# The first transform of a four-layer spectral network on row tiles instead of column tiles of TensorE

## What is computed

```python
# x: (2, 64, 64, 384) float32; four layers, one after the other
x = _L0_conv_ref(x, L0_conv_w1, L0_conv_b1, L0_conv_w2, L0_conv_b2)
x = _L1_conv_ref(x, L1_conv_ln1_g, ..., L1_conv_mlp_b2)
x = _L2_conv_ref(x, L2_conv_w1r, ..., L2_conv_b2)
x = _L3_conv_ref(x, L3_conv_w1, ..., L3_conv_b2)

def _L0_conv_ref(x, w1, b1, w2, b2):          # 8 heads of 48 channels; layers 2 and 3 are of this kind
    xs = jnp.fft.rfft2(x, axes=(1, 2))
    xs = xs.reshape(B, H, W // 2 + 1, 8, 48)
    xr, xi = jnp.real(xs[:, lo:hi, :wk]), jnp.imag(xs[:, lo:hi, :wk])
    o1r = relu(einsum('bxyhi,hio->bxyho', xr, w1[0]) - einsum('bxyhi,hio->bxyho', xi, w1[1]) + b1[0])
    o1i = relu(einsum('bxyhi,hio->bxyho', xi, w1[0]) + einsum('bxyhi,hio->bxyho', xr, w1[1]) + b1[1])
    ...                                        # a second complex product, with w2 and b2
    out = softshrink(zr, 0.01) + 1j * softshrink(zi, 0.01)
    return jnp.fft.irfft2(out, s=(H, W), axes=(1, 2)) + x

def _L1_conv_ref(x, ln1_g, ln1_b, ln2_g, ln2_b, w1, b1, w2, b2, mlp_w1, mlp_b1, mlp_w2, mlp_b2):
    h = _ln(x, ln1_g, ln1_b)                   # layer norm over the channels
    h = afno2d(h, w1, b1, w2, b2) + x          # as above, first 32 of 64 rows of modes, gelu, no shrinking
    m = _ln(h, ln2_g, ln2_b)
    return _gelu(m @ mlp_w1 + mlp_b1) @ mlp_w2 + mlp_b2 + h
```

## Time and profile before

| | us |
|---|---|
| median of 3 runs | 2166.53 |
| lowest, highest | 2162.26, 2170.68 |
| the profiled execution's own time | 2166.18 |
| its span | 2164.1 |

### The profile page before, as it was taken

One profiled execution on the slowest core, in us unless ns is written; L12 is line 12 of the kernel. 1 busy time (PEld: TensorE's weight loads), 2 busy tenths in 40 slices (PEclk: granted clock), 3 DMA queues, 4 the chain that ended last, 5 costly groups with the idle time before them and its releaser, 6 DMA issues.

```text
span 2164.1 us, 76669 instructions
## 1 busy us (share of the span) xinstructions
PE 2056.5 (95%) x35424; PEld 1766.8 (82%) x35424; DVE 937.7 (43%) x1814; ACT 874.2 (40%) x1470; POOL 440.4 (20%) x425
## 2 busy tenths in 40 slices
PE   5999995999998999999999999999999999999997
PEld 4788873887885999999999999998787888877885
DVE  1354667875645433333333333331343443433443
ACT  2544445443443333333333333333444444444442
POOL 3211013975521110000000000001220220221200
PEclk9999997999999999999999999999999999999999
DMA  9425638306425111111111111114707257246314
GB/s 163 89 45 82 113 58 148 54 18 109 113 60 135 30 30 30 29 29 29 29 29 29 29 29 29 39 35 84 110 5 122 49 83 118 58 76 116 61 23 99
DMA packets 299726, 141.57 MB, mean 65 GB/s; under 512 B 275632, under 2 KB 298032, under 8 KB 299440
## 3 DMA queue, kind: packets, MB, share of 16 engines
q1 hardware_dynamic: 299440, 137.11, 34.9%
HBM read 74.17 MB, written 62.91 MB: 63 GB/s over the span
## 4 chain that ended last, share of the span: by engine, by line
PE 92%; DVE 3%; issue 2%; DMA 1%; SPq 1%; ACT 1%; POOL 0%; DVEq 0%; ACTq 0%; POOLq 0%
PE ps L578 19%; PE ps L563 19%; PE ps L466 11%; PE ps L436 10%; PE ps L450 9%; PE ps L485 8%; PE ps L420 8%; PE ps L500 7%; PE ps L548 1%; DMA xs<-in_x 1%; DMA wraw<-in_w 1%; DVE xn L827 1%; DVE st L807 1%; DVE mv L812 0%; DVE xn L829 0%
## 5 line engine op out<-in xcount | busy, mean ns | idle before, releaser
L436 PEld LDWEIGHTS ps<-const,z 128*48 128x48 f32 x8384 | 286.6, 124 | 102.5 <-issue 72.0
L910 DVE TENSOR_TENSOR gl<-g,gh 128x512 fp32r<-128x512 f32 x192 | 156.9, 817 | 476.5 <-ACT gh L719 476.5
L716 ACT ACTIVATE g<-ps,colp 128x512 f32<-128x512 f32 x192 | 132.4, 689 | 529.4 <-PE ps L563 529.4
L770 DVE TENSOR_SCALAR clamp<-ps 128x384 f32<-128x384 f32 (+1 forms) x216 | 113.2, 524 | 529.4 <-PE ps L466 529.3
L466 PE MATMUL ps<-w,h 113*64 113x48 f32 (+1 forms) x8384 | 285.4, 218 | 15.7 <-issue 14.4
L436 PE MATMUL ps<-const,z 128*48 128x64 f32 (+1 forms) x8384 | 283.3, 218 | 6.7 <-issue 4.6
L660 ACT ACTIVATE h<-ps,w 113x512 f32<-113x512 f32 (+2 forms) x280 | 171.1, 611 | 290.2 <-PE ps L450 290.2
L466 PEld LDWEIGHTS ps<-w,h 113*64 113x64 f32 (+1 forms) x8384 | 260.0, 131 | 23.0 <-issue 18.5
L420 PE MATMUL ps<-const,xn 128*64 128x64 f32 x6144 | 226.9, 228 | 45.3 <-POOL xn L996 21.2
L578 PE MATMUL ps<-w2h,gh 128*128 128x384 f32 x768 | 261.9, 341 | 0.0
L450 PE MATMUL ps<-zf,w 112*49 112x512 f32 (+5 forms) x1120 | 260.4, 528 | 0.6 <-issue 0.5
(11 more groups left out here) (67 smaller groups left out, 2392.9 us busy)
## 6 DMA issues: line engine op xcount, KB each, us to landing
after<-xs SPq DMA_DIRECT2D x96, 384.0 KB, 5.4
xs<-after SPq DMA_DIRECT2D x94, 384.0 KB, 8.8
after<-om SPq DMA_DIRECT2D x32, 384.0 KB, 4.3
out<-xs SPq DMA_DIRECT2D x32, 384.0 KB, 5.5
xm<-after SPq DMA_DIRECT2D x30, 384.0 KB, 6.3
xs<-in_x SPq DMA_DIRECT2D x24, 384.0 KB, 8.6
wstage<-in_spectral SPq DMA_DIRECT2D x16, 210.0 KB, 7.2
xs<-in_x SPq DMA_DIRECT2D x4, 768.0 KB, 11.6
```

What stands on the lines that cost most here:

```text
L436: mm = pe.matmul(ps[a * SIDE:a * SIDE + BLOCK, F2_BANK, n * L.kh:(n + 1) * L.kh], z[:, g % 2, slot, :], basis(col + a * SIDE, L.kh), start ...
L716: act.activation(g[:, n % 2, :], ps[:, MM1_BANKS[n % 2], :], ACT.Gelu, bias=colp[:, n:n + 1]).then_inc(g_ready, 1)
L910: dve.tensor_tensor(gl[:, n % 4, :], g[:, n % 2, :], gh[:, n % 4, :], ALU.subtract).then_inc(g_low, 1)
```

## The change

Two chunks of 8 channels become one *twin* of 16, three a group. The stationary tile is now 64 partitions (one image) x 128 columns (two channels, 64 rows h each); the moving operand is the 64 table columns on the same 64 partitions. The two images are two row tiles, which write banks 0 and 1 over all 128 partitions. The table `d1` is no longer block-diagonal: it is 64 columns, given once for each image. A twin has 16 matmuls; two chunks had 32.

The result has other places: partitions (channel parity j, h), columns (channel pair c, part a, k), bank b. `z` stays as it was, so ScalarE sorts: four copies of 64 partitions x 512 for a twin, of which two move data to the other half of the partitions. Each copy reads both banks, so the next `f1` waits for all four of the twin before. `f1_at` becomes [1, 4, 7] ([1, 4, 6] in layer 1); VectorE's `centre` keeps the old six places under the name `centre_at`.

```diff
@@ -30,6 +30,8 @@
 SPAN = BATCH * HALF
 CHAN = 8
 CHUNKS = BLOCK // CHAN
+TWINS = CHUNKS // 2
+SPREAD = 4
 ROWCHUNK = 8
 ROWCHUNKS = SIDE // ROWCHUNK
 PARTS = 4
@@ -40,7 +42,8 @@
 STATS = PAIRS + 1
 
 SIGNS = 5
-C_D1, C_D2, C_D2A, C_D2B, C_SIGN = [P * n for n in range(5)]
+C_D1 = 0
+C_D2, C_D2A, C_D2B, C_SIGN = [SPAN + P * n for n in range(4)]
 C_ID, C_D5, C_D5H, C_D6, C_COLS = [C_SIGN + SIGNS + P * n for n in range(5)]
 ROWS = ONE_ROW + 1
 MIX = SIDE + BLOCK
@@ -63,7 +66,8 @@
         self.groups = list(zip(starts, sizes))
         self.n = len(sizes)
 
-        self.f1_at = [0, 1, 3, 5, 7, 8] if self.full else [0, 1, 3, 4, 6, 7]
+        self.f1_at = [1, 4, 7] if self.full else [1, 4, 6]
+        self.centre_at = [0, 1, 3, 4, 6, 7]
         self.f5_at = [2, 3, 4, 5, 6, 7] if self.full else [1, 2, 3, 4, 5, 6]
 
     def column(self, slot):
@@ -406,26 +410,30 @@
             def f1(g, k):
 
                 L = layer_of(g)
-                n = CHUNKS * g + k
+                n = TWINS * g + k
+                chunk = 2 * n + 1
                 if L.norm and g == BLOCKS:
                     pe.wait_ge(rows_ready, SIDE)
                 elif L.norm:
-                    pe.wait_ge(xn_ready, n - CHUNKS * (BLOCKS + 1) + 1)
+                    pe.wait_ge(xn_ready, chunk - CHUNKS * (BLOCKS + 1) + 1)
                 else:
-                    pe.wait_ge(xt_ready, n + 1 - (CHUNKS * BLOCKS if L.index > 1 else 0))
-                if n >= 2:
-                    pe.wait_ge(z_ready, n - 1)
+                    pe.wait_ge(xt_ready, chunk + 1 - (CHUNKS * BLOCKS if L.index > 1 else 0))
+                if n >= 1:
+                    pe.wait_ge(z_ready, SPREAD * n)
                 for c in range(CHAN):
-                    for a in range(2):
-                        mm = pe.matmul(ps[a * SIDE:(a + 1) * SIDE, F1_BANKS[n % 2], c * SPAN:(c + 1) * SPAN],
-                                       xn[:, n % RING, c, :], basis(C_D1 + a * SPAN, SPAN), start=True, stop=True)
+                    slot, first = (chunk - 1 + c // (CHAN // 2)) % RING, c % (CHAN // 2) * 2
+                    for b in range(BATCH):
+                        rows = slice(b * SIDE, (b + 1) * SIDE)
+                        mm = pe.matmul(ps[:, F1_BANKS[b], c * SPAN:(c + 1) * SPAN],
+                                       xn[rows, slot, first:first + 2, :].rearrange("p c h -> p (c h)"),
+                                       const[rows, C_D1:C_D1 + SPAN], start=True, stop=True)
                 mm.then_inc(f1_done, 1)
 
             def f2(g, t):
 
                 L = layer_of(g)
                 if t == 0:
-                    pe.wait_ge(z_ready, CHUNKS * (g + 1))
+                    pe.wait_ge(z_ready, SPREAD * TWINS * (g + 1))
                     if g == 0:
                         pe.wait_ge(s_second, 16)
                         pe.wait_ge(gap_clear, 1)
@@ -504,7 +512,7 @@
 
             def spectral(first, last):
 
-                for k in range(CHUNKS):
+                for k in range(TWINS):
                     f1(first, k)
                 for g in range(first, last):
                     L = layer_of(g)
@@ -610,16 +618,19 @@
 
             def f1(g, k):
 
-                n = CHUNKS * g + k
-                act.wait_ge(f1_done, n + 1)
-                act.activation(z[:, g % 2, :, k * CHAN:(k + 1) * CHAN],
-                               ps[:, F1_BANKS[n % 2], :].rearrange("p (c s) -> p s c", s=SPAN),
-                               ACT.Copy, scale=layer_of(g).forward).then_inc(z_ready, 1)
+                act.wait_ge(f1_done, TWINS * g + k + 1)
+                for j, a in ((0, 0), (0, 1), (1, 1), (1, 0)):
+                    mine, to = slice(j * SIDE, (j + 1) * SIDE), slice(a * SIDE, (a + 1) * SIDE)
+                    first = 2 * k * CHAN + j
+                    act.activation(z[to, g % 2, :, first:first + 2 * CHAN - 1:2].rearrange("p (k b) c -> p k b c", b=BATCH),
+                                   ps[mine, F1_BANKS[0]:F1_BANKS[1] + 1, :]
+                                   .rearrange("p b (c a k) -> p a k b c", a=2, k=HALF)[:, a],
+                                   ACT.Copy, scale=layer_of(g).forward).then_inc(z_ready, 1)
 
             def normalise_row(r):
 
                 if r == 0:
-                    act.wait_ge(f1_done, CHUNKS * BLOCKS)
+                    act.wait_ge(f1_done, TWINS * BLOCKS)
                     act.wait_ge(x_loaded[buffer_of(PAIRS)], LOADS * (uses_before(PAIRS) + 1))
                 if r % ROWCHUNK == 0:
                     act.wait_ge(rstd_ready, r // ROWCHUNK + 1)
@@ -853,8 +864,8 @@
                             m2(g, t - 1)
                         elif g > first:
                             m2(g - 1, layer_of(g - 1).n - 1)
-                        if norm and t in L.f1_at:
-                            n = CHUNKS * (g + 1 - first) + L.f1_at.index(t) + AHEAD
+                        if norm and t in L.centre_at:
+                            n = CHUNKS * (g + 1 - first) + L.centre_at.index(t) + AHEAD
                             if n < CHUNKS * (last - first):
                                 centre(n)
                         if norm and 0 <= L.n * (g - last + 2) + t - 4 < HC:
@@ -992,14 +1003,14 @@
                         pool.wait_ge(x_loaded[buffer_of(unit)], LOADS * (uses_before(unit) + 1))
                 n = CHUNKS * g + k
                 if n >= RING:
-                    pool.wait_ge(f1_done, n - RING + 1)
+                    pool.wait_ge(f1_done, (n - RING) // 2 + 1)
                 pool.tensor_copy(xn[:, n % RING], channels(g, k)).then_inc(xt_ready, 1)
 
             def keep(n):
 
                 g, k = BLOCKS + n // CHUNKS, n % CHUNKS
                 data, channel = channels(g, k), n * CHAN
-                pool.wait_ge(f1_done, CHUNKS * BLOCKS + n + 1)
+                pool.wait_ge(f1_done, TWINS * BLOCKS + n // 2 + 1)
                 scale = lnrow[:, 0, channel:channel + CHAN].unsqueeze(2).to_broadcast([P, CHAN, SIDE])
                 pool.tensor_tensor(xn[:, n % RING], xn[:, n % RING], scale, ALU.mult).then_inc(gained, 1)
                 pool.wait_ge(gained, n + 1)
@@ -1072,7 +1083,7 @@
     col = np.stack([np.cos(f * np.outer(n, half)), -np.sin(f * np.outer(n, half))], 1)
     col[:, 1, 0] = (-1.0) ** n
 
-    d1 = np.einsum("wak,bd->bwakd", col, np.eye(BATCH)).reshape(P, 2 * SPAN)
+    d1 = np.tile(col.reshape(SIDE, SPAN), (BATCH, 1))
 
     inv = 2 * col.transpose(1, 2, 0)
     inv[:, 0] /= 2
```

## The result

| | us |
|---|---|
| before, median of 4 runs | 2167.07 |
| changed, median of 4 runs | 2227.09 (2223.43 to 2228.49) |
| ratio | 1.0276, 95% interval 1.0252 to 1.0299 |
| span of the profiled executions | 2164.1 before, 2225.0 after |

The account below looks back on a forecast made before the run. TensorE was taken to bound the kernel, with f1's pace set by weight loads. The terms -8 + 20 + 4 + 5 + 18 = +39 us on 2166.2 us gave 2205 us, range 2116 to 2240, likeliest case 2178 to 2238.

Parts of the forecast that it names:

- Pace of f1: Steady f1 on TensorE: 55 ns a record with row tiles' loads side by side, 1.77 us a twin, -8 us.
- The slow end: Upper end for an f1 record on TensorE: 108 ns, each weight load waiting for the last.
- the quick load: Rival for f1's weight load: it does not grow with columns, pace stays 29.1 ns, 2124 us; chance 0.19.
- Changes of shape: Around f1 on TensorE: 153 tile-shape changes at 0.13 us, +20 us, and the longer first load, +4 us.
- both terms together: f1's blocks with the shape changes around them: -8 + 24 = 16 us.
- Steps without f1: Steps 0 and 8 of full groups, where only m2 covers f2, copy zf, m1: 0.10 us each, +5 us.
- ScalarE: The four sorting copies a twin, 0.598 us each, delay v and h but cost nothing, hidden by TensorE's length.
- Starts: Segment starts, f1 against its copies without cover: first record to f2 13 to 18 us, +18 us in all.
- loads one behind the other: Rival for f1: row tiles' weight loads run in sequence, 108 ns a record, 2364 us; chance 0.12.
- ScalarE as the bound: Rival: sorting copies of 1.2 us make h and v late, some 1 us at 87 places, 2290 us; chance 0.07.

Follow-up runs that it names:

- the one-tile run: Changed kernel with a twin's 16 matmuls ordered by image, eight of one row tile, then eight of the other: 2408.2 us in a single execution.
- the banks: Changed kernel with the second twin of the f1 run at each segment's start sent to banks 6 and 7: 2210.9 us, ratio 1.0208.
- four tiles: Changed kernel with f1 on tiles of 64 x 64, each channel a stationary tile of its own, 32 matmuls a twin: 2166.8 us, ratio 1.0005.
- the small matmul on the same shape: Kernel before, plus one matmul of 8 moving columns on a 128 x 64 tile ahead of each f1 chunk: 2179.3 us, ratio 1.0056.
- the other shape: Kernel before, plus one matmul of 8 moving columns, stationary 64 rows x 128 columns, ahead of each f1 chunk: 2223.4 us, ratio 1.0263.
- all three: Changed kernel with f1 on 64 x 64 tiles, f1 at steps 1, 4, 6 (layer 1: 1, 4, 5), banks 6 and 7 at starts: 2143.2 us, ratio 0.990.
- without the banks: Changed kernel with f1 on 64 x 64 tiles and at steps 1, 4, 6 (layer 1: 1, 4, 5): 2153.9 us, ratio 0.9946.
- the steps: Changed kernel with f1 at steps 1, 4, 6 instead of 1, 4, 7 (layer 1: 1, 4, 5): 2209.9 us, ratio 1.0199.

## Why the prediction was right, and what it had wrong

*Pace of f1*: right. 55.7 ns for 55; the one-tile run shows that the load sets it and that two row tiles load side by side. The slow end, 108 ns, is nearly what the kernel without turns does (101 ns); the quick load, 29.1 ns, was seen on no tile with 128 stationary columns.

*Changes of shape*: right. 0.10 to 0.13 us on going in, 0.15 (with the first long load) on coming out; 15 us for the 16 of both terms together. The 0.13 us themselves were not measured apart from the long load.

*Steps without f1*: 8 us for 5 (22 x 2 x 0.10 is 4.4). At step 0 of layer 1, which I had left out, `m2` grew by 0.27 us.

*ScalarE*: the failed step, in the sentence that `v` "is needed by the next `f5` chunk, over 3 us later". That is so at steps 1 to 6. The last chunk, at step 7 (6 in layer 1), is followed by no `f5` but by `f6` of the same group at the last step, which needs all six chunks; there `v` has only `m2` and `m1` to hide behind. The order of TensorE was known; I had looked for `v`'s reader in the same stage alone. It cost 25 us by the times of the last step; the run that moves `f1` from step 7 takes the wait away, and the kernel is 17 us faster by it. The sentence that `m2(t)` asks for `h` only behind `f6`, `f2` and `f5` of the next step fails as well, where there is no `f6` and `f5`: in the first group of each segment, 7.2 us in eight waits. In the table those of the first segment are part of the 8.4 us; in the other two segments nearly as much idle time went as they brought.

*Starts*: mis-sized, 30 us for 18. The span was put at 13 to 18 us and was 19, as all three twins ran at the slow pace; and nearly nothing came back: 2.7 us of the first start's 11.1, nothing in the second. The idle time that was to be regained did go, 3.7 us for `xn` in the first segment and 2.0 in the second, but `m2`'s waits for `h` took its place with 2.4 and 2.3 us, and in the first group of layer 1 the granted clock was lower (0.82 for 0.94). Against the wait, 16 us were regained by the banks.

*The rest*: the time of the steady groups above their medians fell by 18 us, mostly idle time of PE without a releaser. No term had this, and it was luck: without it the kernel would have come out at some 2245 us, above the range's upper end of 2240. The way from the forecast to the result is so one missed term (+25), one too small (+12), one more of 3, one less of 1, and one unforeseen relief (-18). The range was also drawn narrower than its own terms allow: their bounds, added up, give 2166 to 2245, not 2178 to 2238, and the chances named for slower add up to 0.75, not 0.73. The rival with a quick load falls with the pace; loads one behind the other fall as well; of ScalarE as the bound, the wait at the last step is a part, at one place instead of three, with copies of 0.64 us and not 1.2.

## What to carry to other kernels

Where the weight load sets the pace, halving the matmuls by doubling the stationary columns gained next to nothing here (0.08 us of 1.86 a twin); count columns loaded per tile, and try as many tiles as the shape allows: four 64 x 64 tiles did in 1.09 us what two 64 x 128 did in 1.93. Price each change of tile shape among other stages, here 0.35 us for in and out, the long loads with it. When one copy becomes four in a queue, look up the reader of everything queued behind it at each step of the order, the last ones and those of the first group, where the cover is missing, above all, and give a run without cover a second pair of banks.

## What was not expected of the hardware

A record every 14.7 ns with four tiles, under any pace seen before.

PE stands idle for 1 to 3 us at some places with no releaser, mostly while a unit's loads fill the DMA queues: of the 24 such times over 0.7 us in the kernel before, the DMA share is 0.97 to 1.32 in 18, and 0.10 to 0.18 in 6. The kernel before, in two stretches with such a stall and one without (columns as above):

```profile
262.00:265.00 3.00, 2.05 (x61) 1.84 (x59) 0.89 (x2) 1.03 (x2) 0.00 (x0) 1.00 1.28 184
268.00:272.00 4.00, 2.51 (x85) 2.39 (x81) 0.23 (x1) 1.20 (x2) 0.00 (x0) 1.00 1.31 184
280.00:290.00 10.00, 10.00 (x267) 8.12 (x263) 3.85 (x6) 4.67 (x8) 1.42 (x3) 1.00 0.01 3
```

Summed over the whole trace it is 38 us before, 34 with the small matmul on the same shape, 33 with four tiles, 32 with all three and 37 without the banks; these are the versions with a full group of 39.3 us or less. In those with 39.4 or more it is 9 in the change, 10 with the steps, 7 with the banks, 5 with one row tile at a time and 15 with the other shape. So a version that slows the steady groups loses less than its stages say, and one that speeds them up gives part of the gain back. What PE waits for there, the supply of instructions for one, stays open; no run was made on it.
